# Attention with float32r score stacks in two row halves, and a normalisation moved from ScalarE to GpSimd

## The chip, the cores and the metric

The kernel runs on one core of a Trainium2 chip. The metric is the time of one execution on the device in microseconds (us), as the median of several runs. The engines are named as the profile names them: PE is TensorE (PEld its weight loads), DVE is VectorE, ACT is ScalarE, POOL is GpSimd, and SP is the engine that issues almost all DMAs of this kernel (SPq in the rows).

## The reference

Four blocks follow one another on x of shape (32, 256, 128), each as x = x + block(layernorm(x)): retention, a mixture of 16 experts with one shared, softmax attention, and a block that routes 63 tokens of each sequence through attention and an FFN. The change is in the third block and at the edge of the fourth:

```python
h = _layernorm(x, axis=-1)                 # x: 32 sequences x 256 tokens x 128
q = (h @ Wq.T + bq).reshape(b, s, 16, 8) * 8 ** -0.5
k = (h @ Wk.T + bk).reshape(b, s, 16, 8)
v = (h @ Wv.T + bv).reshape(b, s, 16, 8)
probs = softmax(einsum('bqhd,bkhd->bhqk', q, k))
x = x + einsum('bhqk,bkhd->bqhd', probs, v).reshape(b, s, 128) @ Wo.T + bo
h3 = _layernorm(x, axis=-1)                # input of the last block
```

## The kernel before, in words

`attention_phase` handles the 32 sequences in a software pipeline that is written out by hand: each engine has a list of steps with lags, and in turn `it` it runs each step of its list for sequence `it - lag`. All engines work in order, so the order of a list is the order of the work, and semaphores hold a step until its inputs are there.

A head has only 8 values, so a score matmul would use 8 of the 128 rows of the PE array. The kernel uses the rows for precision instead. `split_qk` on POOL cuts q and k into three bfloat16 parts (four dependent operations for each of q and k). `store_parts` writes the parts to DRAM and `fill(half)` reads them back into `q_stack` and `k_stack`, one row for each pair of parts and each of the 8 values: 72 rows, for 8 heads (a half) at a time. One bfloat16 matmul on 72 rows then gives the score of a head. It is computed twice. `for_maximum(j)`, called m0 to m7 below, computes four heads with queries on the partitions, and DVE reduces them to the negated maximum. `split_max` cuts the maximum into three parts, `transpose_max` turns it, `copy_maxT` takes it from PSUM, and `give_max` writes it as three more rows under `q_stack`, against rows of ones under `k_stack`. `for_exponential(j)`, e0 to e7, then gives score minus maximum with keys on the partitions, on 75 rows, and ACT takes the exponential. `values(g)`, V0 to V3, multiplies with v in four column strips of the array.

Per sequence SP issues 11 DMAs: four stores of parts, four fills, two maxima and the output. `q_stack` and `k_stack` have two buffers (p is 0 or 1), and a fill for sequence s waits until the e steps of the same half of sequence s - 2 are done, and until the parts of s are stored. PE waits for the fills at m0 (half 0) and m4 (half 1), and for the maxima at e0 and e4.

One turn of PE's list is: e6, v, m7, e7, V2, m0, oT, e0, m1, y, e1, m2, max1, V3, h, e2, m3, e3, token, V0, m4, qk, m5, e4, m6, max0, V1, e5. Here v, qk and y are projections, h, oT and token are transposes, and max0 and max1 are `transpose_max`.

SP's list of one turn:

```python
pipeline(sp, [(fill(1), 4), (fill_ones, 4), (store_parts, 3), (store_out, 9), (give_max(1), 5),
              (fill(0), 3), (give_max(0), 4), (load_later, 0)], B, B)
```

At the end of a sequence `inv_std3` on POOL computes the scale and shift of the next layernorm, `norm3` on ACT applies them (two ACTIVATEs of 128x128), and `weigh` on POOL uses the result.

Of the kernel before, what the change touches and what calls it, by code (L numbers as in the profile page):

```python
# [10 lines left out]
BF16 = mybir.dt.bfloat16  # L11
I32 = mybir.dt.int32
U32 = mybir.dt.uint32
ALU = mybir.AluOpType
# [987 lines left out]
PARTS = 3  # L1002
PAIRS = PARTS * PARTS
QK_ROWS = PAIRS * AD
EXP_ROWS = QK_ROWS + PARTS
UNIT = 4
M_UNITS = AH // UNIT * TPS
# [25 lines left out]
def attention_phase(nc, w, keep, out):  # L1033


    with Memory(nc) as m:
# [8 lines left out]
        ident_b = m.sbuf("a_ident_b", [P, P], BF16)  # L1045
# [3 lines left out]
        ones_b = m.sbuf("a_ones_b", [PARTS, S], BF16)  # L1049
# [10 lines left out]
        rest = m.sbuf("a_rest", [P, 2, S])  # L1060
        part = m.sbuf("a_part", [P, 2, 2, PARTS, S], BF16)
        SLOTS = 2 * PARTS + PARTS - 1
        part_dram = nc.dram_tensor("part_dram", (2, HALVES, SLOTS, AD, HH, S), BF16, kind="Internal").ap()
        q_stack = m.sbuf("a_q_stack", [P, 2, HALVES, HH, S], BF16)
        k_stack = m.sbuf("a_k_stack", [P, 2, HALVES, HH, S], BF16)
        v_tok = m.sbuf("a_v_tok", [P, 2, TPS, D])
        v_pad = m.sbuf("a_v_pad", [P, 2, TPS, AH, APAD])
        neg_max = m.sbuf("a_neg_max", [P, 2, HALVES, TPS, HH])
        max_rest = m.sbuf("a_max_rest", [P, TPS, HH])
        max_part = m.sbuf("a_max_part", [P, HALVES, TPS, PARTS, HH], BF16)  # L1070
        max_T = m.sbuf("a_max_T", [PARTS * HH, HALVES, S], BF16)
# [65 lines left out]
        h3_done = m.sem("e_h_done")  # L1137
        product_done = m.sem("e_product_done")
# [8 lines left out]
        FILLS = 2  # L1147
# [5 lines left out]
        def _(sp):  # L1153
# [8 lines left out]
            def fill_ones(s, p, r):  # L1162
                if s == 0:
                    sp.wait_ge(preset, 4)
                    for q in range(2):
                        for half in range(HALVES):
                            sp.dma_start(k_stack[QK_ROWS:EXP_ROWS, q, half],
                                         ones_b[:].unsqueeze(1).to_broadcast([PARTS, HH, S])).then_inc(ones_in, 16)

            def store_parts(s, p, r):  # L1170
                slots = lambda half, first, end: part_dram[p, half, first:end].rearrange("a d h s -> (d h) a s")
                rows = lambda half: part[half * HH * AD:(half + 1) * HH * AD, p].rearrange("r w a s -> r (w a) s")
                after(sp, part_step, 8 * s + 4)
# [5 lines left out]
                for half in range(HALVES):  # L1179
                    sp.dma_start(slots(half, 0, 2 * PARTS), rows(half)).then_inc(part_stored[p][half], 16)  # L1180
# [1293 lines left out]
```

## Time and profile before

| what | value |
|---|---|
| median of 3 runs | 1086.14 us (1085.76 to 1087.13) |
| the profiled execution | 1087.2 us, span of its instructions 1085.4 us |
| attention phase, first m0 to last e | 482.8 to 960 us of the span |
| busy over the whole span | PE 88%, DVE 65%, POOL 65%, ACT 59% |
| PE clock granted, mean | 0.949 of full speed |

The span is what the profile shows from the first to the last instruction. Busy shares are means over four phases with different limits. For this change only the attention phase counts, and in it the stretch in which the pipeline is full.

### The profile page before, as it was taken

To read this page: it belongs to the slowest core of one execution; us is meant where nothing else is said; L and a number is where in the kernel's file an instruction comes from. 1 tells how busy PE (TensorE), PEld (TensorE's weight loads), DVE (VectorE), ACT (ScalarE), POOL (GpSimd) and SP (SyncE) were. 2 spreads that over 40 slices of the span, in tenths; PEclk is the share of its full clock that TensorE was granted. 3 is DMA by queue.
4 is the path that set the end of the run, shared out by engine and by line. 5 is a ranking of instruction groups with operands and counts; after the bars stand their busy time and mean duration, and the time that the engine had idled before them with its cause. 6 is when DMAs were issued, how large, how long until landed. Compare 5 with 4: busy or idle time off the path is not lost. (4 is left out here: it accounts for less than half of the span.)

```text
span 1085.4 us, 29610 instructions
## 1 busy us (share of the span) xinstructions
PE 956.3 (88%) x9809; PEld 706.1 (65%) x9810; DVE 704.7 (65%) x1509; ACT 641.7 (59%) x1304; POOL 703.8 (65%) x1531
## 2 busy tenths in 40 slices
PE   6999997669899999449999999999999999954675
PEld 5888886458777666335767777777777777623554
DVE  5888887634444444237788777778878777825752
ACT  4777775311124433125788888888888888752551
POOL 4777775466625555467688888888888887544003
PEclk9999999789999999757999999999999999987999
DMA  8600000311122332134344544454454444302000
GB/s 319 252 3 3 3 3 2 121 45 42 42 70 82 82 84 65 44 109 132 116 140 138 149 127 140 125 147 137 139 141 129 125 124 128 102 16 61 7 3 20
DMA packets 88836, 100.90 MB, mean 93 GB/s; under 512 B 10654, under 2 KB 74366, under 8 KB 88318
## 3 DMA queue, kind: packets, MB, share of 16 engines
q1 hardware_dynamic: 83454, 87.98, 27.5%
q0 software_dynamic: 5248, 11.15, 3.2%
q8 instruction: 82, 1.34, 0.5%
q14 instruction: 52, 0.43, 0.1%
HBM read 61.79 MB, written 36.47 MB: 91 GB/s over the span
## 5 line engine op out<-in xcount | busy, mean ns | idle before, releaser
L1367 DVE TENSOR_REDUCE a_neg_max<-a_slot 128x4 f32<-128x1024 f32 x256 | 306.7, 1219 | 109.0 <-PE a_slot L1510 84.3
L1455 ACT ACTIVATE a_pT<-a_slot 128x1024 f32<-128x1024 f32 x256 | 255.4, 1024 | 14.0 <-PE a_slot L1526 7.1
L1510 PE MATMUL a_slot<-a_k_stack,a_q_stack 72*128 72x256 bf16 x1024 | 158.3, 279 | 7.3 <-DMA a_k_stack<-part_dram 6.5
L1526 PE MATMUL a_slot<-a_q_stack,a_k_stack 75*128 75x256 bf16 x1024 | 150.8, 275 | 2.6 <-ACT a_pT L1455 0.7
L1541 PE MATMUL a_ps_o<-a_pT,a_v_pad 128*32 128x256 f32 x2048 | 141.6, 386 | 0.0
L1510 PEld LDWEIGHTS a_slot<-a_k_stack,a_q_stack 72*128 72x128 bf16 x1024 | 95.7, 99 | 51.8 <-issue 25.5
L727 POOL DMA_INDIRECT y_rows<-m_total,m_token x80 | 76.6, 957 | 68.7 <-issue 40.4
L1526 PEld LDWEIGHTS a_slot<-a_q_stack,a_k_stack 75*128 75x128 bf16 x1024 | 92.8, 98 | 36.4 <-ACT a_pT L1455 14.3
L720 POOL DMA_INDIRECT sorted_in<-h,m_slot x64 | 62.6, 978 | 42.5 <-issue 24.0
L330 DVE TENSOR_TENSOR r_score<-ps_score,r_decay 128x512 f32<-128x512 f32 x128 | 81.5, 678 | 7.9 <-PE ps_score L489 7.8
L1541 PEld LDWEIGHTS a_ps_o<-a_pT,a_v_pad 128*32 128x32 f32 x2048 | 64.8, 109 | 27.5 <-issue 13.0
L910 PE MATMUL m_banks<-h2T,shared_up 128*128 (+1 forms) x256 | 65.3, 401 | 16.3 <-ACT m_gate L860 12.0
L829 DVE TENSOR_TENSOR m_hidden_e<-m_gate_e,m_banks 128x512 f32<-128x512 f32 x40 | 27.5, 688 | 76.2 <-issue 60.8
L959 PE MATMUL m_banks<-expert_up,m_xeT 128*128 x160 | 75.4, 593 | 0.3 <-ACT m_xeT L868 0.3
L860 ACT ACTIVATE m_gate<-m_banks 128x512 f32<-128x512 f32 x32 | 19.1, 597 | 86.8 <-PE m_banks L910 39.8
L910 PEld LDWEIGHTS m_banks<-h2T,shared_up 128*128 128x128 f32 x256 | 48.6, 199 | 25.4 <-issue 19.5
L385 ACT ACTIVATE r_h<-x,r_shift,r_rstd 128x128 f32<-128x128 f32 x128 | 56.7, 497 | 12.4 <-POOL r_shift L257 11.9
L776 DVE TENSOR_TENSOR m_hidden<-m_gate,m_banks 128x512 f32<-128x512 f32 x32 | 21.9, 685 | 53.9 <-remote 26.8
L875 ACT ACTIVATE m_gate_e<-m_banks 128x512 f32<-128x512 f32 x40 | 23.9, 598 | 48.5 <-PE m_banks L959 42.1
L255 POOL TENSOR_TENSOR r_rstd<-r_ve,r_half 128x2 f32<-128x2 f32 x64 | 45.3, 707 | 5.0
L1272 POOL TENSOR_TENSOR a_part<-a_qk,a_zeros 128x256 bf16<-128x256 f32 x64 | 39.1, 611 | 11.3 <-ACT a_qk L1441 8.8
L1272 POOL TENSOR_TENSOR a_part<-a_rest,a_part 128x256 bf16<-128x256 f32 x64 | 43.0, 672 | 5.0
(296 smaller groups left out, 2113.6 us busy)
## 6 DMA issues: line engine op xcount, KB each, us to landing
a_q_stack<-part_dram SPq DMA_DIRECT2D x64, 288.0 KB
a_k_stack<-part_dram SPq DMA_DIRECT2D x64, 288.0 KB
part_dram<-a_part SPq DMA_DIRECT2D x64, 192.0 KB, 2.7
sorted_in<-h SPq DMA_DIRECT2D x10, 528.0 KB, 13.0
m_xe<-sorted_in SPq DMA_DIRECT2D x40, 132.0 KB
expert_up<-in_eu_dram SPq DMA_DIRECT2D x1, 4096.0 KB, 24.2
part_dram<-a_part SPq DMA_DIRECT2D x64, 64.0 KB, 3.8
out_dram<-e_x_plus_h SPq DMA_DIRECT2D x32, 128.0 KB, 2.5
```

Of the source, the lines that this page charges most:

```text
L330: nc.vector.tensor_tensor(score[:, p, tile], ps_score[tile][:], own, ALU.mult).then_inc(score_done, 1)
L385: ins = nc.scalar.activation(h[:, p, t], x_sb[:, s * TPS + t, :], ACT.Identity, bias=shift[:, p, t:t + 1], scale=rstd[:, p, t:t + 1])
L720: nc.gpsimd.indirect_dma_start(sorted_in, bass.IndirectOffsetOnAxis(ap=slot[:, t:t + 1], axis=0), h2_all[:, t, :], None).then_inc(scattere ...
L727: nc.gpsimd.indirect_dma_start(y_rows, bass.IndirectOffsetOnAxis(ap=token[:, at:at + 1], axis=0), ye[:, t % RING, j], None).then_inc(store ...
L910: ins = nc.tensor.matmul(bank[2 * which + p][:, f * S:(f + 1) * S], shared_up[:, which, f], h2T_all[:, bass.ds(s * S, S)], start=True, sto ...
L959: ins = nc.tensor.matmul(bank[PAIR * (p % 2) + j], xeT[:, p % 2, j], w_up[:, expert[j]], start=True, stop=True)
L1272: nc.gpsimd.tensor_tensor(to, a, b, op).then_inc(steps, 1)
L1367: nc.vector.tensor_reduce(neg_max[:, p, half, t, g * UNIT:(g + 1) * UNIT], slots[SLOT_OF["m", j]][:], AX.X, ALU.max, negate=True).then_inc ...
L1455: nc.scalar.activation(pT[:, j % PT_RING], slots[SLOT_OF["e", j]][:], ACT.Exp).then_inc(e_read, 1)
L1510: ins = nc.tensor.matmul(slots[SLOT_OF["m", j]][:, q], q_stack[0:QK_ROWS, p, half, head, t * P:(t + 1) * P], k_stack[0:QK_ROWS, p, half, h ...
L1526: ins = nc.tensor.matmul(slots[SLOT_OF["e", j]][:, q], k_stack[0:EXP_ROWS, p, half, head, t * P:(t + 1) * P], q_stack[0:EXP_ROWS, p, half, ...
L1541: ins = nc.tensor.matmul(ps_o[q * APAD:(q + 1) * APAD, g // 2], v_pad[:, p, t, g * UNIT + q], pT[:, (2 * g + t) % PT_RING, q], start=g % 2 ...
```

## The change

- The scores use float32r operands. q and k are cut into two parts instead of three (two POOL operations each instead of four), so that the pairs of parts take 4 x 8 = 32 rows.
- The stacks are float32 and hold two halves of rows. Rows 0 to 63 serve one half of the heads of a group and rows 64 to 127 the other. In each half rows 32 to 61 are filled with zeros on both sides, and rows 62 and 63 hold the two parts of the maximum on the q side and ones on the k side. The m matmuls use 62 rows of a half and the e matmuls 64. The matmuls of a group of four heads alternate between the two row halves, and write two PSUM banks.
- The DRAM scratch is split into `q_dram` and `k_dram`. Per sequence there are six stores of parts, eight fills of 32 rows, four maxima of 2 rows, and the output: 19 DMAs instead of 11.
- The k fill reads its 16 rows twice by an outermost dimension of 2 with step 0. The q fill repeats in an inner dimension, as before.
- `norm3` runs on POOL as two whole-tile operations with broadcast scale and shift.
- The one-off fill of zeros and ones is larger and stands first in SP's list.

```diff
-PARTS = 3
+PARTS = 2
-EXP_ROWS = QK_ROWS + PARTS
+TILES = 2
+TILE_ROWS = P // TILES
+MAX_ROWS = TILE_ROWS - PARTS
+HT = HH // TILES
...
             def fill(half):
                 def step(s, p, r):
                     after(sp, e_filled, ((s - 2) * 4 + 2 * half + 2) * (M_UNITS // 8) * 2)
-                    after(sp, part_stored[p][half], twice(16, r + 1))
-                    sp.dma_start(q_stack[0:QK_ROWS, p, half],
-                                 part_dram[p, half, 0:PARTS].rearrange("a d h s -> (a d) (h s)").unsqueeze(1)
-                                 .to_broadcast([PARTS * AD, PARTS, HH * S])).then_inc(filled[p][half], 16)
-                    sp.dma_start(k_stack[0:QK_ROWS, p, half],
-                                 bass.AP(part_dram.tensor, part_dram[p, half, PARTS].offset,
-                                         [[HH * S, PARTS * AD], [AD * HH * S, PARTS], [1, HH * S]])
-                                 ).then_inc(filled[p][half], 16)
+                    after(sp, part_stored[p][half], 16 * STORES * (r + 1))
+                    for tile in range(TILES):
+                        rows, heads = slice(tile * TILE_ROWS, tile * TILE_ROWS + QK_ROWS), slice(tile * HT, (tile + 1) * HT)
+                        sp.dma_start(q_stack[rows, p, half],
+                                     q_dram[p, half, :, :, heads].rearrange("a d h s -> (a d) (h s)").unsqueeze(1)
+                                     .to_broadcast([PARTS * AD, PARTS, HT * S])).then_inc(filled[p][half], 16)
+                        sp.dma_start(k_stack[rows, p, half],
+                                     k_dram[p, half, :, :, heads].rearrange("d a h s -> (d a) (h s)").unsqueeze(0)
+                                     .to_broadcast([PARTS, PARTS * AD, HT * S])).then_inc(filled[p][half], 16)
...
+            def scores(slot, rows, weights, moving, of_weights, p, half, g):
+                for r in range(UT):
+                    for tile in range(TILES):
+                        at = slice(tile * TILE_ROWS, tile * TILE_ROWS + rows)
+                        ins = nc.tensor.matmul(slot[:, tile * UT + r], weights[at, p, half, g * UT + r, of_weights].bitcast(F32R),
+                                               moving[at, p, half, g * UT + r].bitcast(F32R), start=True, stop=True)
...
+            def norm3(s, p, r):
+                after(pool, shift3_done, s + 1)
+                h3 = given[:, bass.ds(s * TPS, TPS), 0:D]
+                over_d = lambda a: a[:, p].unsqueeze(2).to_broadcast([P, TPS, D])
+                nc.gpsimd.tensor_tensor(h3, x_sb[:, bass.ds(s * TPS, TPS), :], over_d(rstd3), ALU.mult).then_inc(scaled3, 1)
+                after(pool, scaled3, s + 1)
+                nc.gpsimd.tensor_tensor(h3, h3, over_d(shift3), ALU.add).then_inc(h3_done, 1)
```

SP's instructions for one turn in the full pipeline, from `fill(1)` to `give_max(0)`; first before (sizes are partitions x repeats x elements):

```order
L1187 DMA a_q_stack<-part_dram 72x1x2048
L1190 DMA a_k_stack<-part_dram 72x1x2048
L1176 DMA part_dram<-a_part 64x2x256 x2
L1180 DMA part_dram<-a_part 64x6x256 x2
L1206 DMA out_dram<-e_x_plus_h 128x2x128
L1199 DMA a_q_stack<-a_max_T 3x8x256
```

The turn goes on with the same fills for half 0 and one more maximum. And after the change, the whole turn:

```order
L1198 DMA a_q_stack<-q_dram 32x1x1024
L1201 DMA a_k_stack<-k_dram 32x1x1024
L1198 DMA a_q_stack<-q_dram 32x1x1024
L1201 DMA a_k_stack<-k_dram 32x1x1024
L1184 DMA k_dram<-a_part 8x8x256 x4
L1188 DMA q_dram<-a_part 64x2x256 x2
L1219 DMA out_dram<-e_x_plus_h 128x2x128
L1211 DMA a_q_stack<-a_max_T 2x4x256 x2
L1198 DMA a_q_stack<-q_dram 32x1x1024
L1201 DMA a_k_stack<-k_dram 32x1x1024
L1198 DMA a_q_stack<-q_dram 32x1x1024
L1201 DMA a_k_stack<-k_dram 32x1x1024
```

Each fill of a half has become four issues, the stores six, and each maximum two, all in the same place of the turn; a pair of maxima follows as before.

POOL's instructions for one turn, from the bias to the output, before:

```order
L1237 TENSOR_TENSOR x<-x,a_bo 128x256
L1300 TENSOR_TENSOR a_v_pad<-a_v_tok,a_zeros 128x4x4x8 x2
L1252 TENSOR_TENSOR e_shift<-e_minus_mean,e_rstd 128x2
L1272 TENSOR_TENSOR a_max_part<-a_neg_max,a_zeros 128x2x8
L1272 TENSOR_TENSOR a_max_rest<-a_neg_max,a_max_part 128x16
L1272 TENSOR_TENSOR a_max_part<-a_max_rest,a_zeros 128x2x8
L1272 TENSOR_TENSOR a_max_part<-a_max_rest,a_max_part 128x2x8
L1311 TENSOR_TENSOR e_product<-h,d_rw 128x256
```

And after:

```order
L1251 TENSOR_TENSOR x<-x,a_bo 128x256
L1313 TENSOR_TENSOR a_v_pad<-a_v_tok,a_zeros 128x4x4x8 x2
L1266 TENSOR_TENSOR e_shift<-e_minus_mean,e_rstd 128x2
L1324 TENSOR_TENSOR h<-x,e_rstd 128x2x128
L1326 TENSOR_TENSOR h<-h,e_shift 128x2x128
L1284 TENSOR_TENSOR a_max_part<-a_neg_max,a_zeros 128x4x4
L1286 TENSOR_TENSOR a_max_part<-a_neg_max,a_max_part 128x4x4
L1332 TENSOR_TENSOR e_product<-h,d_rw 128x256
```

The two operations of `norm3` (on `h`) have come in right behind the shift, and the split of a maximum has two operations instead of four. The order of the matmul groups on PE is the same in both kernels.

## Rows read from the trace of the kernel before

**Rows 1.** The page, part 1: busy time of each engine.

```profile
PE 956.3 (88%) x9809; PEld 706.1 (65%) x9810; DVE 704.7 (65%) x1509; ACT 641.7 (59%) x1304; POOL 703.8 (65%) x1531
```

**Rows 2.** Windows, full pipeline: stretch, length, engines' busy us, PE clock, DMA share, GB/s.

```profile
641.20:935.60 294.40, 293.63 (x3054) 207.85 (x3057) 236.27 (x391) 243.76 (x418) 250.09 (x590) 1.00 0.48 134
```

**Rows 3.** Groups of DVE and POOL instructions in 641.2 to 935.6 us.

```profile
L1367 DVE TENSOR_REDUCE a_neg_max<-a_slot 128x4 f32<-128x1024 f32 x161 | 192.9, 1219 | 57.7 <-PE a_slot L1510 41.4 <-POOL a_max_part L1272 15.0
L1377 DVE TENSOR_TENSOR a_o_tok<-a_ps_misc,a_inv_sum 128x256 f32<-128x256 f32 x20 | 8.5, 424 | 0.7
...
L1311 POOL TENSOR_TENSOR e_product<-h,d_rw 128x256 f32<-128x256 f32 x20 | 14.5, 726 | 1.6
```

**Rows 4.** Timeline of PE inside one turn: start us, length us, engine, line.

```profile
707.07 0.60 PE L1510 MATMUL a_slot<-a_k_stack,a_q_stack 72*128 72x256 bf16 x4
707.50 0.60 PE L1526 MATMUL a_slot<-a_q_stack,a_k_stack 75*128 75x256 bf16 x4
...
710.59 0.59 PE L1596 MATMUL a_ps_misc<-a_hT,a_wk 128*128 128x256 f32 x2
711.02 0.60 PE L1510 MATMUL a_slot<-a_k_stack,a_q_stack 72*128 72x256 bf16 x4
```

**Rows 5.** Timeline of PE in the retention phase, with a matmul group in row strips.

```profile
101.86 0.38 PE L527 MATMUL ps_tail<-ident,r_h 128*128 128x128 f32 x2
102.17 1.15 PE L489 MATMUL ps_score<-r_qT,r_kT 32*128 32x256 f32 x16
103.24 1.08 PE L504 MATMUL ps_turns<-r_score,r_v_pad 128*32 128x128 f32 x32
```

**Rows 6.** Timeline of POOL: a split of q, of which two steps stand here.

```profile
703.30 0.61 POOL L1272 TENSOR_TENSOR a_part<-a_qk,a_zeros 128x256 bf16<-128x256 f32 x1
704.00 0.67 POOL L1272 TENSOR_TENSOR a_rest<-a_qk,a_part 128x256 f32<-128x256 f32 x1
...
706.19 0.73 POOL L1237 TENSOR_TENSOR x<-x,a_bo 128x256 f32<-128x256 f32 x1
```

**Rows 7.** Timeline of SP's DMA issues in one turn.

```profile
701.19 0.79 SPq L1187 DMA_DIRECT2D a_q_stack<-part_dram  x1
...
703.51 1.31 SPq L1176 DMA_DIRECT2D part_dram<-a_part  x2
706.14 1.24 SPq L1180 DMA_DIRECT2D part_dram<-a_part  x2
707.42 0.65 SPq L1206 DMA_DIRECT2D out_dram<-e_x_plus_h  x1
708.13 0.79 SPq L1199 DMA_DIRECT2D a_q_stack<-a_max_T  x1
709.03 0.84 SPq L1187 DMA_DIRECT2D a_q_stack<-part_dram  x1
709.92 0.77 SPq L1190 DMA_DIRECT2D a_k_stack<-part_dram  x1
```

**Rows 8.** Waits of SP in 641.2 to 935.6: us in total, times, longest.

```profile
SPq L1199 <- ACT a_max_T L1447: 45.1, 20, 2.7
SPq L1180 <- POOL a_part L1272: 36.2, 20, 1.9
SPq L1187 <- PE a_slot L1526: 32.9, 21, 1.9
```

**Rows 9.** Issues of 128-partition loads at the program's start: min/median/max ns.

```profile
L221 SPq DMA_DIRECT2D x<-in_x_dram x4: 398/432/432, 0.8 to 7.8; - x4
```

**Rows 10.** Windows with full DMA queues: a 128-partition load, then fills alone.

```profile
20.00:25.00 5.00, 5.00 (x80) 4.15 (x69) 4.60 (x16) 2.90 (x8) 1.92 (x7) 1.00 1.04 418
479.20:479.40 0.20, 0.00 (x0) 0.00 (x0) 0.00 (x0) 0.06 (x1) 0.20 (x2) 0.50 0.80 328
```

**Rows 11.** The page, part 3: SP's queue over the span.

```profile
q1 hardware_dynamic: 83454, 87.98, 27.5%
```

**Rows 12.** Line 1176, the smaller store of parts.

```profile
DMA to landing us min/median/max: 2.2/3.8/5.0
```

More of the change, by code:

```diff
@@ L1170, in store_parts @@
             def store_parts(s, p, r):
-                slots = lambda half, first, end: part_dram[p, half, first:end].rearrange("a d h s -> (d h) a s")
-                rows = lambda half: part[half * HH * AD:(half + 1) * HH * AD, p].rearrange("r w a s -> r (w a) s")
-                after(sp, part_step, 8 * s + 4)
+                rows = lambda half, which: part[half * HH * AD:(half + 1) * HH * AD, p, which]
+                after(sp, part_step, 2 * PARTS * s + PARTS)
                 for half in range(HALVES):
@@ L1175, in store_parts @@
                     after(sp, filled[p][half], twice(8 * FILLS, r))
-                    sp.dma_start(slots(half, 2 * PARTS, SLOTS), rows(half)[:, PARTS:2 * PARTS - 1]
+                    for a in range(PARTS):
+                        sp.dma_start(k_dram[p, half, :, a], rows(half, 1)[:, a]
+                                     ).then_inc(part_stored[p][half], 16)
+                after(sp, part_step, 2 * PARTS * (s + 1))
+                for half in range(HALVES):
+                    sp.dma_start(q_dram[p, half].rearrange("a d h s -> (d h) a s"), rows(half, 0)
@@ L1177, in store_parts @@
                                  ).then_inc(part_stored[p][half], 16)
-                after(sp, part_step, 8 * (s + 1))
-                for half in range(HALVES):
-                    sp.dma_start(slots(half, 0, 2 * PARTS), rows(half)).then_inc(part_stored[p][half], 16)
             def fill(half):
@@ L1280, in step @@
                         for half in range(HALVES):
-                            after(pool, part_stored[p][half], twice(16, r))
-                    split(part_step, 8 * s + 4 * n, qk[:, p, which], rest[:, which], part[:, p, which, 0],
-                          part[:, p, which, 1], part[:, p, which, 2], [P, S])
+                            after(pool, part_stored[p][half], 16 * STORES * r)
+                    split(part_step, 2 * PARTS * s + PARTS * n, qk[:, p, which], part[:, p, which, 0], part[:, p, which, 1], [P, S])
                 return step
@@ L1632, in by_half @@
 def by_half(weight):
-    return np.ascontiguousarray(weight.reshape(-1, HALVES, HH, AD).transpose(0, 1, 3, 2).reshape(-1, D))
+    heads = weight.reshape(-1, HALVES, HH // UNIT, TILES, UT, AD)
+    return np.ascontiguousarray(heads.transpose(0, 1, 5, 3, 2, 4).reshape(-1, D))
 def by_pair(rows):
```

120 lines of the change are left out of this document (57 added, 63 removed).

## The prediction

> **What bounds the kernel now.** I read the page's busy times first: PE leads with 88% [rows 1]. That is a mean over four phases, so the next view is the windows of the stretch in which the attention pipeline is full. In 294.4 us PE is busy 293.6 us at full clock, POOL 250.1, ACT 243.8, DVE 236.3, and the DMA engines 48% [rows 2]. The groups of the same stretch contain exactly 20 multiplications of `a_o_tok`, one per sequence [rows 3], so one turn takes 294.4 / 20 = 14.72 us. Per turn PE is busy 14.68 us, POOL 12.5, ACT 12.2, DVE 11.8. DVE's reduction of the maxima waited 41.4 us for PE [rows 3]: PE ends last, and the others follow. SP is not in those columns. Its own waits add up to 45.1 + 36.2 + 32.9 = 114.2 us over the 20 turns, 5.7 us each [rows 8], so its 11 issues take the other 9.0 us. SP is an in-order engine with 5.7 us to spare, and the change gives it 19 issues.
>
> **The change part by part.**
>
> *PE, less work in the scores.* A bfloat16 group of four heads takes 0.44 us from its start to the next group's [rows 4], and a turn has 16 of them. No float32r matmul is in the trace. Its lower bound is the bfloat16 price, its upper bound that of float32: there a matmul of 256 columns, in two records, takes 0.43 us [rows 4] where bfloat16 takes 0.11. That row strips run beside each other is shown by the retention scores: 16 float32 records in four strips take 1.07 us until the next group starts [rows 5], where 16 records in sequence at 0.43 / 2 would take 3.4. Two strips thus halve a group: 0.22 us at the bfloat16 rate, 0.86 at the float32 rate. I take the bfloat16 rate, because the kernel cuts the values into parts ahead, as it does for bfloat16 and for no float32 matmul; the saving is 16 x 0.22 = 3.5 us a turn.
>
> The Trainium skill (FP8 and Floating Point Precision, TensorE Precision Notes) says that true float32 takes four passes and that there is a reduced form which reads 4-byte values and truncates them. By it the lower end would hold; no row of this trace shows it.
>
> *PE, more changes of the array's division.* In rows 5 the two transposes (0.22 us, as a record of 128 columns takes 0.43 / 4) last 0.31 us until the strips start: 0.09 us for the change. The strip group takes 1.07 us where four rounds of 0.215 are 0.86, of which 0.09 is the next change and about 0.11 the first weight load, which is hidden nowhere. So a change into 128-column work costs 0.2 us. In PE's list the division changes 8 times a turn before (around the `values` groups, with max0 and max1 in the same strips as V3 and V1), and 18 times after, because each projection or transpose now stands between strip groups. That is 10 x 0.2 = 2.0 us more, and 4 x 0.1 for the float32r load that is now unhidden at the four old changes from `values` back to scores or transposes. PE: 14.7 - 3.5 + 2.0 + 0.4 = 13.6 us.
>
> *POOL.* A split of q lasts from 703.30 to 706.19, 2.9 us, of which the first two operations take 0.70 and about 0.65 [rows 6]. Each of the two splits saves 1.5 us, each split of a maximum about 0.6. `norm3` adds two operations of 0.73 [rows 3] and a wait of 0.08. Net 12.5 - 3.0 - 1.2 + 1.5 = 9.8 us. ACT loses two ACTIVATEs. Both stay under 13.6 us, so these parts move nothing by themselves; the cover is PE's (or SP's) turn, and without it the moved normalisation would cost its 1.5 us.
>
> *SP.* From issue to issue a store takes 0.66 us (1.31 for two), the output 0.71, a maximum 0.90, a fill 0.89 [rows 7]. After: 6 x 0.66 + 0.71 + 4 x 0.90 + 8 x 0.89 = 15.4 us a turn. The lower bound takes the q fills at the price of plain loads, 0.43 us [rows 9], plus a gap of 0.05: 4 x 0.41 less, 13.8 us. SP no longer has its 5.7 us, and behind each issue stand all later fills and maxima, for which PE waits at m0, m4, e0 and e4.
>
> *The fills' spread.* This term decides. When only fills are queued, the DMA engines are 80% busy and move 328 GB/s, where a load of 128 partitions fills them (1.04) and moves 418 [rows 10]. The fills' 72 rows begin with a dimension of 24, and 0.8 of 16 engines is about 12, half of 24. So a fill is not spread over all engines, and what it is spread over follows its dimensions, not its bytes. The new k fill's source begins with a dimension of 2 (the repeat with step 0). If the outermost dimension limits the spread, two engines carry the 32 rows of 4 KB, the same two for each k fill. The bounds are 16 engines and 2. I take 2, as the dimension is nearest to that.
>
> The Trainium skill (DMA: Bandwidth & Descriptors, "Why a DMA increments its semaphore by 16 and not by 1") states this as a rule: the number of engines is the largest up to 16 that divides the slowest dimension of both access patterns. By it the fills of before have 12 engines, with which the trace's 0.80 agrees, and the new k fills 2, the lowest-numbered. That speaks against this change.
>
> *Price with two engines.* 328 GB/s over 12 engines are 27.3 bytes per ns, so a 4 KB row takes 0.15 us and a k fill 16 x 0.15 = 2.4 us. The page gives the slow bound: 87.98 MB in 27.5% of 16 engines' 1085.4 us are 18.4 bytes per ns [rows 11], 3.6 us a k fill. The pair's ring is in order, so the loop of one turn is: both k fills of half 1 with the q rows between, 5.1 us; the stores issued behind them, about 1.2; their completion, 0.8; SP sees `part_stored` and issues a q and a k fill of half 0, 1.8; start-up, 0.8; the k fills of half 0, 5.1; q rows and the maxima behind them, 0.6; semaphores and gaps, 0.5. Start-up plus completion is 1.6 because a small store lands 2.2 us after an issue of 0.63 at best [rows 7, 12]. Sum 15.9 us. At the slow price each of four k fills costs 1.2 more: 20.6 us.
>
> **Sum.** The loop (15.9) is longer than SP's issues (13.8 to 15.4) and PE's work (13.6). A turn grows by 1.2 us, 32 turns by 39 us. Ahead of the first m0 the fills are 3 us slower and two splits 3 us faster: nothing. The profiled execution took 1087.2 us, of which 1085.4 is span; 1087.2 + 39 = 1126, and the median of the runs lies 1.1 us lower: 1125. I round up to 1127, as every in-order wait of SP adds to the loop.
>
> **The rivals.**
> - *Wide spread, cheap issues: faster.* If a k fill runs on four or more engines, it takes at most 1.2 us and the loop falls below SP's time. With q fills issued at 0.43 us the turn is SP's 13.8 with a little waiting, 13.9: 32 x 0.8 = 26 us less, about 1060; with still cheaper issues PE's 13.6, 1050. For it: nothing in the trace shows a repeat dimension in front. Against: the 0.80 share, and SP's sum. It decides at an SP turn of 14.7 us. Chance 0.17; a tie within 0.2% (2 us, what a measurement of this kernel can tell from no change), a turn of 14.66 to 14.78, has 0.04.
> - *Wide spread, SP's issues at full price.* The turn is 15.4 us: 32 x 0.7 = 22, 1108. Chance 0.10.
> - *float32r is not at the bfloat16 rate.* At half of it PE's turn is 13.6 + 3.5 = 17.1, 1163; at the float32 rate 13.6 + 16 x 0.64 = 23.8, 1377. Chances 0.08 and 0.05.
> - *PE's clock falls in the new waits.* While PE stood idle before m0 the granted clock was 0.50 [rows 10], and 1.00 in the full pipeline [rows 2]. With a turn of 15.9 PE waits 2.3 us, in pieces at m0, e0 and e4. If half of each turn ran at half clock, 13.6 would become 20.4: 1270. Short waits speak against. Chance 0.04.
>
> **The numbers.** The narrow loop has 0.52, with its own range from 1108 (SP's full price) to 1175 (part of the rows at the slow price). Predicted 1127 us. The range goes from 1065 to 1190: it leaves out the lower half of the fast rival and, above, the float32 rate, the clock and the slow end of the loop, 0.2 together. Faster 0.17, same 0.04, slower 0.79.
>
> **What would show it.** SP's waits nearly gone but for `part_stored` and the e steps; a DMA share that falls though the bytes stay; PE idle before m0 and e0 with the k fill or the maximum as releaser; groups of four heads 0.22 us apart; DVE and ACT less busy per turn. I am wrong if a full-pipeline turn is under 14.7 us, if PE waits for nothing and still takes longer, or if the score groups take 0.4 us or more.

## The result and the profile after

The changed kernel takes 1207.46 us (median of 4 runs, 1200.32 to 1220.06), the kernel before 1086.64 on the same chip. The ratio is 1.108, with a 95% interval of 1.102 to 1.114: slower by 121 us where 41 were predicted, and above the range (1190). The ratio leaves out the slowest of the four, 1220.06 us, which is the profiled one; its mean granted clock, 0.899, is that of the other three (0.896 to 0.902), so its rows are used for where the time goes and the ratios for how much.

The page, part 1 and the largest idle times of part 5 (columns after the bar: busy us and mean ns, idle us ahead of the group and its releaser):

```profile
PE 982.5 (81%) x9810; PEld 686.2 (56%) x9810; DVE 708.4 (58%) x1508; ACT 619.8 (51%) x1240; POOL 633.0 (52%) x1340
...
L1387 DVE TENSOR_REDUCE a_neg_max<-a_slot 128x4 f32<-128x1024 f32 x256 | 308.1, 1221 | 211.3 <-PE a_slot L1518 204.4
...
L1518 PE MATMUL a_slot<-a_k_stack,a_q_stack 62*128 62x256 f32 x1024 | 129.7, 338 | 93.0 <-DMA a_k_stack<-k_dram 91.2
```

PE is busy for longer than before [rows 1] although its matmuls were to become shorter, and it waits 93 us ahead of the m groups, nearly all of it for the k fill. DVE, whose work is the same [rows 3], now waits 204 us for PE.

The window of the full pipeline, which is [rows 2] for the kernel before, and the multiplication of `a_o_tok` in it, one per sequence (number, durations in ns, first and last start):

```profile
535.50:1071.00 535.50, 446.03 (x4408) 277.29 (x4400) 344.15 (x563) 330.93 (x542) 292.50 (x668) 0.91 0.33 99
```

```profile
L1397 DVE TENSOR_TENSOR a_o_tok<-a_ps_misc,a_inv_sum x30: 424/424/426, 535.5 to 1071.0; 128x256 f32<-128x256 f32 x30
```

A turn takes 535.5 / 29 = 18.47 us on average, in place of 14.7. (The median execution is 12.6 us shorter than the profiled one; if the difference lies in the 32 turns, its turn is 0.4 us less, by estimate 18.1.) PE is busy 15.38 us of it and idle 3.09, and its clock, 1.00 before, is 0.91. The average hides a pattern. The starts of that multiplication in a row, from DVE's timeline:

```profile
759.36 0.42 DVE L1397 TENSOR_TENSOR a_o_tok<-a_ps_misc,a_inv_sum 128x256 f32<-128x256 f32 x1
773.83 0.42 DVE L1397 TENSOR_TENSOR a_o_tok<-a_ps_misc,a_inv_sum 128x256 f32<-128x256 f32 x1
796.60 0.42 DVE L1397 TENSOR_TENSOR a_o_tok<-a_ps_misc,a_inv_sum 128x256 f32<-128x256 f32 x1
811.09 0.42 DVE L1397 TENSOR_TENSOR a_o_tok<-a_ps_misc,a_inv_sum 128x256 f32<-128x256 f32 x1
834.23 0.42 DVE L1397 TENSOR_TENSOR a_o_tok<-a_ps_misc,a_inv_sum 128x256 f32<-128x256 f32 x1
```

14.5, 22.8, 14.5, 23.1 us: every second turn is as fast as before the change, and the other loses 8. What the slow one is made of stands in windows of PE (length, busy us, granted clock, DMA share, GB/s) and in two rows of its timeline:

```profile
780.00:782.50 2.50, 2.50 (x32) 1.00 0.22 57
782.50:785.00 2.50, 0.71 (x16) 1.00 0.35 107
785.00:787.50 2.50, 0.67 (x5) 0.94 0.39 120
787.50:790.00 2.50, 2.50 (x14) 0.50 0.64 180
790.00:792.50 2.50, 2.50 (x20) 0.50 0.30 98
792.50:795.00 2.50, 2.50 (x29) 0.70 0.16 53
```

```profile
786.83 0.50 PE L1518 MATMUL a_slot<-a_k_stack,a_q_stack 62*128 62x256 f32 x4 [3.62 <-DMA a_k_stack<-k_dram]
...
791.86 1.93 PE L1553 MATMUL a_ps_o<-a_pT,a_v_pad 128*32 128x256 f32 x16
```

PE works without a pause until 783, stands still for 3.62 us ahead of m0 until the k fill has landed, and goes on. Only then does the clock fall, from 1.00 to 0.50 (from 2.4 to 1.2 GHz). The windows' clocks put it at 0.50 for 0.3 + 5.0 + 1.5 = 6.8 us. A group of values that takes 1.07 us elsewhere takes 1.93 there. So the slow turn pays twice, once for the wait and once for what the wait does to the clock. A wait of 1.38 us for the other half's k fill, ahead of the m4 at 812.71, leaves the clock at 1.00. Why slow and fast turns alternate is not shown. The half speed may give the transfers time to catch up, but it is not needed for it: in `warm6` below, turns of 16.0 and 19.0 us alternate in places where the clock did not fall.

### The profile page after: what moved, and what is told of

Its sections match the earlier page's. It is cut to its first block and busy times, and to the rows that moved or that the text cites. A ratio compares the mean times of both kernels' runs of the same rounds, so it can differ in the third digit from the quotient of the medians.

```text
span 1218.2 us, 29542 instructions
## 1 busy us (share of the span) xinstructions
PE 982.5 (81%) x9810; PEld 686.2 (56%) x9810; DVE 708.4 (58%) x1508; ACT 619.8 (51%) x1240; POOL 633.0 (52%) x1340
## 3 DMA queue, kind: packets, MB, share of 16 engines
q8 instruction: 82, 1.34, 0.5%
## 5 line engine op out<-in xcount | busy, mean ns | idle before, releaser
L1518 PE MATMUL a_slot<-a_k_stack,a_q_stack 62*128 62x256 f32 x1024 | 129.7, 338 | 93.0 <-DMA a_k_stack<-k_dram 91.2
L1518 PEld LDWEIGHTS a_slot<-a_k_stack,a_q_stack 62*128 62x128 f32 x1024 | 89.3, 214 | 136.9 <-DMA a_k_stack<-k_dram 103.0
L1553 PE MATMUL a_ps_o<-a_pT,a_v_pad 128*32 128x256 f32 x2048 | 146.2, 406 | 0.0
L1518 PE MATMUL a_slot<-a_q_stack,a_k_stack 64*128 64x256 f32 x1024 | 124.6, 335 | 14.0 <-DMA a_q_stack<-a_max_T 11.1
L1518 PEld LDWEIGHTS a_slot<-a_q_stack,a_k_stack 64*128 64x128 f32 x1024 | 82.2, 202 | 51.4 <-issue 23.3
L1313 POOL TENSOR_TENSOR a_v_pad<-a_v_tok,a_zeros 128x128 f32<-128x128 f32 x64 | 24.2, 398 | 155.6 <-PE a_ps_o L1553 155.6
L1553 PEld LDWEIGHTS a_ps_o<-a_pT,a_v_pad 128*32 128x32 f32 x2048 | 55.7, 114 | 52.9 <-issue 28.6
L386 ACT ACTIVATE r_h<-x,r_shift,r_rstd 128x128 f32<-128x128 f32 x128 | 56.7, 497 | 12.4 <-POOL r_shift L258 11.9
L1284 POOL TENSOR_TENSOR a_max_part<-a_neg_max,a_zeros 128x16 fp32r<-128x16 f32 x64 | 13.7, 213 | 91.8 <-DVE a_neg_max L1387 91.8
L1460 ACT ACTIVATE a_qk<-a_ps_misc,a_bq_scaled 128x256 f32<-128x256 f32 x32 | 15.2, 474 | 76.9 <-PE a_ps_misc L1608 76.9
L1488 ACT COPY a_oT<-a_ps_misc 128x256 f32<-128x256 f32 x32 | 11.9, 372 | 74.9 <-PE a_ps_misc L1622 74.6
```

What stands on the lines that cost most here:

```text
L386: ins = nc.scalar.activation(h[:, p, t], x_sb[:, s * TPS + t, :], ACT.Identity, bias=shift[:, p, t:t + 1], scale=rstd[:, p, t:t + 1])
L1313: ins = nc.gpsimd.tensor_tensor(own_columns(v_pad[:, p].rearrange("p t h e -> p (t h) e"), g), v_tok[:, p].rearrange("p t (a g q e) -> p ( ...
L1518: ins = nc.tensor.matmul(slot[:, tile * UT + r], weights[at, p, half, g * UT + r, of_weights].bitcast(F32R), moving[at, p, half, g * UT + ...
L1553: ins = nc.tensor.matmul(ps_o[q * APAD:(q + 1) * APAD, g // 2], v_pad[:, p, t, g * UNIT + q], pT[:, (2 * g + t) % PT_RING, q], start=g % 2 ...
```

## The experiments

Theory A, formed on these rows: each k fill is carried by two of the 16 DMA engines, their ring makes the fills late, and the clock comes on top. Theory B: SP's 19 issues in order are the bound. Theory C: the float32r groups in row strips make the clock fall by themselves. All ratios are to the kernel before on the same chip. Times in us that an expectation names are on the scale of the first chip (1086.64 us for before), so a ratio is what they are held against. The kernels ran on more than one chip: before takes 1065 to 1066 us on three of them and 1089 on the fourth (that of the second set), hence the ratios. Its turn is the same [rows 2] (14.68 in `before_here`). Kernels of the same turn end their first turn at 497 us on the one and at 515 on the other, so the difference lies ahead of the attention. In the kernel before and its regrouped control, whose code is the same up to there, it lies in one place: the 64 transfers to `sorted_in` in the mixture of experts start at 207.5 and 208.0 us, and the last starts at 307.4 in `before_here`, on the slower chip, and at 290.4 in `before_regroup`. Why is open.

**wide.** Part k0 is stored twice in DRAM, so that the k fill needs no repeat.

```diff
-k_dram = nc.dram_tensor("k_dram", (2, HALVES, AD, PARTS, HH, S), F32, kind="Internal").ap()
+k_dram = nc.dram_tensor("k_dram", (2, HALVES, PARTS + 1, AD, HH, S), F32, kind="Internal").ap()
...   # the two k stores of a half now write slots 0 and 1 in one transfer, and slot 2 (k0) in the other
-    k_dram[p, half, :, :, heads].rearrange("d a h s -> (d a) (h s)").unsqueeze(0)
-    .to_broadcast([PARTS, PARTS * AD, HT * S])).then_inc(filled[p][half], 16)
+    bass.AP(k_dram.tensor, k_dram[p, half, 0, 0, tile * HT].offset,
+            [[HH * S, PARTS * AD], [AD * HH * S, PARTS], [1, HT * S]])).then_inc(filled[p][half], 16)
```

> The changed kernel with the same number of issues, bytes and semaphores, but the part k0 is stored twice in DRAM (slots k0, k1, k0), so that the source of each k fill begins with a dimension of 16 instead of 2 and has no repeat. Theory A (narrow ring: two DMA engines carry each k fill, PE waits for it in every second turn and then runs at half clock): both the waits and the half clock go; a turn falls from 18.6 to between 13.6 and 14.7 us, 1050 to 1087 us in all. Theory B (SP's 19 issues in order are the bound, the spread is harmless): nothing changes, 1200 to 1215. Theory C (the score groups in row strips by themselves make the clock fall, whoever waits): the k fill waits go but the clock stays near 0.9, 1150 to 1190.

Measured: 1063.18 us, ratio 0.999 (0.9975 to 1.0007). The window of its full pipeline:

```profile
497.35:903.60 406.25, 391.91 (x4210) 246.36 (x4204) 327.91 (x541) 316.51 (x525) 284.57 (x646) 1.00 0.48 134
```

A turn is 14.65 us and the clock 1.00. SP has the same 19 issues, and the groups are the same: A holds, B and C fall. The edit also touches the k stores: their targets begin with a dimension of 64 in place of 8, and two of the four carry twice the bytes. That the k fill's source counts, and not the stores, is shown by the next two kernels: `both_narrow` keeps the new stores and has the loss, and `split` keeps the old ones, and PE waits for the k fill only 3.3 us in 430 in its weight loads, where it was 89.1 in 535.5.

**both_narrow.** From `wide`, the first two source dimensions of both fills exchanged:

```diff
-    [[HH * S, PARTS * AD], [AD * HH * S, PARTS], [1, HT * S]]
+    [[AD * HH * S, PARTS], [HH * S, PARTS * AD], [1, HT * S]]
```

> As the first kernel of this set, but with the two source dimensions exchanged in both fills, so that the q fill too begins with a dimension of 2: same bytes, same issues, eight fills a turn on two engines instead of four. Theory A: the pair carries 8 x 2.4 = 19.2 us of rows a turn, with the stores and latencies 22 to 25 us, and PE's half clock on top: 1400 to 1560 us. Theories B and C: no change from the changed kernel, 1200 to 1215.

Measured: 1394.41 us, ratio 1.308 (1.305 to 1.312), which is 1422 us on the expectation's scale, and a turn of 24.9 us, as A said. PE's windows show the ring naked:

```profile
804.00:805.00 1.00, 1.00 (x19) 1.00 0.13 53
805.00:806.00 1.00, 0.26 (x8) 1.00 0.13 53
806.00:807.00 1.00, 0.00 (x0) 1.00 0.13 53
```

The next to last column is the share of 16 engines: 0.13 is two of them, fully busy for microseconds while PE stands still. They move 53 GB/s, 26.5 bytes per ns each, so a row of 4096 bytes takes 0.155 us. The Trainium skill (DMA: Bandwidth & Descriptors, "Why a DMA increments its semaphore by 16 and not by 1") counts the engines by the slowest dimension of both patterns, here 2; the trace agrees.

**split.** The other way to a wide source: a k fill as two transfers of 16 rows.

```diff
-sp.dma_start(k_stack[rows, p, half], ... .unsqueeze(0).to_broadcast([PARTS, PARTS * AD, HT * S]))
+for n in range(PARTS):
+    sp.dma_start(k_stack[rows.start + n * PARTS * AD:rows.start + (n + 1) * PARTS * AD, p, half], ...)
```

> The changed kernel with each k fill cut into two transfers of 16 rows, one for each repeat, so that the source begins with a dimension of 16; four issues a turn more (23 in place of 19). Theory A: SP issues 12.2 + 4 x 0.6 = 14.6 us a turn, which is now the longest: 1075 to 1110 us. Theory B: four more issues make it worse, 1207 + 32 x 2.4, about 1280. Theory C: 1150 to 1200.

Measured: 1103.27 us, ratio 1.039 (1.032 to 1.047), 1129 us on the expectation's scale: far from B's 1280, but above A's range. The turn is 15.85 us, since SP with 23 issues is now the bound. These are all its waits over 27 turns:

```profile
SPq L1198 <- PE a_slot L1519: 15.4, 18, 3.4
SPq L47 <- DMA q_dram<-a_part: 0.5, 1, 0.5
```

SP works 15.3 us a turn, not 14.6. The cost of its issues is a rival to be taken seriously, but it decides at 23 of them, not at 19.

**norm_alone.** The kernel before with only `norm3` on GpSimd:

```diff
-for t in range(TPS):
-    ins = nc.scalar.activation(given[:, s * TPS + t, 0:D], x_sb[:, s * TPS + t, :], ACT.Identity, ...)
+nc.gpsimd.tensor_tensor(h3, x_sb[:, bass.ds(s * TPS, TPS), :], over_d(rstd3), ALU.mult).then_inc(scaled3, 1)
+after(pool, scaled3, s + 1)
+nc.gpsimd.tensor_tensor(h3, h3, over_d(shift3), ALU.add).then_inc(h3_done, 1)
```

> The kernel before with only the second part of the change: the normalisation ahead of the experts on GpSimd. All theories: POOL's 12.5 us a turn becomes 14.0, still under PE's 14.7, and nothing moves: 1084 to 1090 us. Rival: POOL at 14.0 hands its splits on late and PE waits for them: the 1.5 us show in every turn, up to 1135.

Measured: 1089.94 us, ratio 1.024 (1.022 to 1.027). The expectation fell and its rival held: a turn takes 15.6 us, 0.9 of the 1.5 us more, for instance 15.66 from 704.09 to 719.77 in POOL's timeline, and POOL never waits in it:

```profile
704.09 0.61 POOL L1312 TENSOR_TENSOR h<-x,e_rstd 128x256 f32<-128x256 f32 x1
704.78 0.61 POOL L1314 TENSOR_TENSOR h<-h,e_shift 128x256 f32<-128x256 f32 x1
...
719.77 0.61 POOL L1312 TENSOR_TENSOR h<-x,e_rstd 128x256 f32<-128x256 f32 x1
```

```profile
561.50:925.00 363.50, 346.43 (x3541) 240.69 (x3537) 276.93 (x464) 264.80 (x442) 323.17 (x746) 1.00 0.44 128
```

The window gives POOL 323.17 us busy in 363.50, or 13.9 a turn, and yet it is full. The missing 1.7 us are gaps of about 0.08 us between operations that wait for one another, as 704.70 to 704.78 here, which no wait is put down to. In the kernel before, POOL's 12.5 us [rows 2] plus such gaps are by this estimate 14.2 of 14.7: the cover was half a microsecond, not two.

**before_here, wide_act, four_stores_act, four_stores_pool.** The first is the kernel before, for a trace on the second chip. The second is `wide` with `norm3` back on ScalarE, as before the change. The third and fourth also store the parts of a half with two transfers instead of three, as before the change; they differ in the place of `norm3`.

```diff
-for a in range(PARTS): sp.dma_start(k_dram[...], ...)   # and q_dram, three stores for each half
+sp.dma_start(slots(half, 2 * PARTS, 2 * PARTS + 1), rows(half)[:, PARTS:PARTS + 1])   # k0 again
+sp.dma_start(slots(half, 0, 2 * PARTS), rows(half))                                   # q0 q1 k0 k1
```

> The kernel before, unchanged, for a trace of it from the chip of these runs: the ratio is 1.00 by any theory. The last set measured 1065 us for it, the runs shown at first 1086. If the difference lies in the phases ahead of the attention, its turn is 14.6 to 14.7 us here too, and the first turn ends near 497 us in place of 518.

> The changed kernel with the wide k fills (k0 stored twice) and the normalisation ahead of the experts back on ScalarE: the stacks' half of the change alone, mended. Theory A (POOL's own chain has room again once the splits are short): the normalisation's place does not matter here, a turn of 14.5 us as with the wide fills, ratio 0.996 to 1.001. Rival (POOL's two extra operations still delay the splits): a turn of 14.2 us, ratio 0.985 to 0.992.

> As the kernel with wide fills and the normalisation on ScalarE, with q and k parts stored by one transfer for each half as before (4 store issues a turn, not 6; 17 issues in all). With wide fills SP's 12.2 us of issues and its waits chain into the maxima that PE waits for (e0, 0.4 us in most turns). If SP's in-order list is what keeps the turn at 14.5 where PE needs 14.0: a turn of 14.1 to 14.3, ratio 0.985 to 0.993. If PE's work in row strips is the bound: no change against wide_act.

> The whole change, mended: wide k fills, four stores, the normalisation on GpSimd as in the change. In the kernel before that move by itself cost 2.4%, since POOL's list, 12.5 us busy and some 1.7 us of gaps, had under 0.5 us to spare. Here the splits are 4.2 us shorter. If that is the whole reason: as four_stores_act, 0.990 to 0.997. If the move also costs through the order of POOL's list: 1.000 to 1.010.

Measured: `before_here` 1085.8 us. `wide_act` 0.9995 (0.997 to 1.002). `four_stores_act` 0.994 (0.991 to 0.996), `four_stores_pool` 0.993 (0.991 to 0.996). `wide_act` and `wide` do not differ, nor do the last two: the place of `norm3` does not matter once the splits are short. With 17 issues the mended change is faster than the kernel before by 0.6 to 0.7%, which is small, but the intervals leave out 1. The windows of `four_stores_act`:

```profile
517.36:895.00 377.64, 366.12 (x3965) 231.16 (x3958) 308.82 (x514) 315.38 (x545) 241.32 (x565) 1.00 0.49 137
```

The turn is 14.48 us, with PE busy 14.04 and POOL 9.3. In `wide_act` it is 14.70. So SP's list took 0.2 us a turn, but the turn of 14.1 to 14.3 that was expected if it were the whole distance to PE's work did not come.

**warm and warm6.** The changed kernel, narrow fills and all, with useless work where PE would stand idle: 12 or 6 float32 multiplications into the free bank of m0, ahead of the wait.

```diff
+free_slot("m", j, s)
+if j == 0:
+    for n in range(12):   # 6 in warm6
+        nc.tensor.matmul(slots[SLOT_OF["m", j]][:, n % UNIT, 0:P], wq[:], wk[:], start=True, stop=True)
 if j % 4 == 0:
     after(pe, filled[p][half], 16 * FILLS * (r + 1))
-free_slot("m", j, s)
```

> The changed kernel with its narrow k fills, and 12 useless float32 multiplications of 128 columns (2.6 us of PE) written to the free bank of m0 ahead of the wait for the fill, so that PE does not stand idle there. If the half clock after the wait of 3.7 us is a real part of the loss: the clock stays at 1.00, the turns no longer alternate between 14.5 and 22.7, each takes 16.5 to 18 us, 1165 to 1190 us at this chip's before of 1086 (ratio 1.06 to 1.10). If the clock is only a by-product and the ring is all: the added work costs its 2.6 us where PE did not wait, ratio 1.13 to 1.16.

> As warm (narrow fills, useless multiplications ahead of m0's wait), with 6 in place of 12, 1.3 us. PE's work is then 14.5 + 1.3 = 15.8 us a turn. If the ring of the narrow fills by itself needs about 15.9 us, as the prediction said, and the clock stays up: turns of 16.0 to 16.6, ratio 1.045 to 1.065. If the ring itself needs more (17 and above): ratio 1.08 to 1.10, with PE waiting for the k fill in each turn. If 1.3 us are too little to keep the clock: alternating turns, 1.09 to 1.12.

Measured: `warm` 1186.47 us, ratio 1.091 (1.089 to 1.094), `warm6` 1.094 (1.088 to 1.099), both with less time than the changed kernel's 1.108 although PE has 2.9 or 1.4 us more to do in each turn. The window and the work itself in `warm`:

```profile
528.50:1014.00 485.50, 468.15 (x4863) 321.34 (x4855) 325.58 (x537) 313.44 (x523) 284.01 (x646) 1.00 0.35 105
```

```profile
711.81 2.94 PE L1530 MATMUL a_slot<-a_wk,a_wq 128*128 128x128 f32 x24
714.68 0.50 PE L1518 MATMUL a_slot<-a_k_stack,a_q_stack 62*128 62x256 f32 x4
```

The clock stays at 1.00, the turns no longer alternate (17.59 us on average), and m0 follows the useless work directly, with the k fill already there, as the expectation's first case said. So the half clock was a real part of the loss, and the narrow fills alone can be served in 17.6 us. In `warm6` the turn averages 17.96 us, and two of its turns, as windows, tell wait and clock apart:

```profile
564.00:583.00 19.00, 15.85 (x172) 10.36 (x164) 11.96 (x20) 11.47 (x20) 10.53 (x25) 1.00 0.32 98
...
635.20:656.60 21.40, 18.62 (x172) 11.76 (x164) 11.96 (x21) 11.70 (x20) 10.87 (x25) 0.84 0.31 90
```

Both have 172 records of PE and about 3 us of idle time. At clock 1.00 they take 15.85 us of PE, at a mean of 0.84 18.62: 2.8 us of clock in one turn. Not every idle stretch costs clock, and its length alone does not decide. These are the waits of two m0:

```profile
628.18 0.50 PE L1518 MATMUL a_slot<-a_k_stack,a_q_stack 62*128 62x256 f32 x4 [2.25 <-DMA a_k_stack<-k_dram]
...
792.89 0.50 PE L1518 MATMUL a_slot<-a_k_stack,a_q_stack 62*128 62x256 f32 x4 [1.69 <-DMA a_k_stack<-k_dram]
```

After the longer one the clock is 1.00 up to 640 us. After the shorter one it is 0.76 on average from 792.9 to 800.0, with half clock from 794.3 on. The changed kernel has one such case too: a wait of 1.65 us ahead of the m0 at 878.18, and a clock of 0.57 from 879 to 883. What else decides was not measured. The expectation for 6 multiplications (16.0 to 16.6 us a turn if the ring needs 15.9) fell. The time lies in both of its other cases, a ring of 17 us and more with a wait for the k fill in nearly every turn, and a clock that falls in some of them.

**serial_strips, one_strip, full_rows.** The last question is PE's own work. All three start from `four_stores_act`.

```diff
-for r in range(UT):            # serial_strips: these two loops exchanged
-    for tile in range(TILES):
-        at = slice(tile * TILE_ROWS, tile * TILE_ROWS + rows)
+        at = slice(0, rows)    # one_strip
+        at = slice(0, P)       # full_rows
```

> four_stores_act with the two loops of a score group exchanged: two matmuls of the first row half, then two of the second, where they alternate else. Same work, same data, same bank writes. If alternating halves run side by side and two of the same half do not, a group inside a run takes 0.35 to 0.44 us in place of 0.24, a turn grows by 16 x 0.1 to 0.2: ratio 1.08 to 1.20. If the saving of a group came from the float32r form and not from the strips: no change from four_stores_act, 0.992 to 0.996.

> four_stores_act with all four matmuls of a score group on the first row half (rows 0 to 61 or 63), so that no two of them can lie side by side; the scores of the other half's heads are left out (the first half's stand in their place). Same count, columns and form. If the saving of a group comes from the two halves side by side: a group inside a run takes 0.44 us in place of 0.24, a turn 14.5 + 16 x 0.2 = 17.7 us, ratio 1.08 to 1.09. If it comes from the float32r form or the smaller number of rows: no change, 0.991 to 0.996.

> four_stores_act with all four matmuls of a score group over all 128 rows, so that the array's division changes only around the values groups, as before; each score is then the sum of two heads', and the maxima are multiplied by 0 (these parts of the computation are left out). A group should take 4 x 0.11 = 0.44 us as in bfloat16 before. If each change of division costs about 0.2 us (2.0 us a turn for ten): one_strip's turn less 2 us, 14.7 to 15.7 us, ratio 1.00 to 1.03. If the changes are nearly free and the strips gain little by themselves: as one_strip, 1.07 or more.

Measured: `serial_strips` 0.991 (0.988 to 0.994), `one_strip` 1.088 (1.085 to 1.091), `full_rows` 1.025 (1.022 to 1.029). The first came out close to what its expectation gave for a saving from the float32r form (0.992 to 0.996). But it does not separate the two, since in it a matmul of the first half can still lie beside the next one of the second. The other two do: `one_strip` has the form and loses the saving. Windows of `one_strip` and of `full_rows` (turns of 17.47 and 15.64 us):

```profile
508.20:962.50 454.30, 454.30 (x3964) 324.88 (x3956) 310.37 (x514) 321.16 (x544) 242.09 (x565) 1.00 0.41 114
```

```profile
496.80:903.00 406.20, 406.20 (x3952) 321.01 (x3948) 306.21 (x511) 318.11 (x542) 240.97 (x562) 1.00 0.46 127
```

PE is never idle in either, so a turn is PE's work. One after the other: from before to `full_rows` (float32r form, float32 transposes of the maxima, no strips) 14.68 to 15.64, +0.96 us; to `one_strip` (the division changes) 17.47, +1.83; to `four_stores_act` (the halves side by side) 14.04 of PE's work, -3.43. Of the first, 16 x 0.04 = 0.64 us lie in the groups, which start 0.48 us apart in `full_rows` (at 682.24, 682.72 and 683.20) where it was 0.44 [rows 4]. With it goes a change in the weight loads, here of `full_rows`:

```profile
L1515 PEld LDWEIGHTS a_slot<-a_q_stack,a_k_stack 128*128 128x128 f32 x1024 | 136.6, 190 | 21.4 <-issue 14.6
```

190 ns for 128 columns. The bfloat16 loads of the unchanged scores take about half of that, here in the page of `norm_alone`:

```profile
L1511 PEld LDWEIGHTS a_slot<-a_k_stack,a_q_stack 72*128 72x128 bf16 x1024 | 96.4, 100 | 51.4 <-issue 25.5
```

The Trainium skill (TensorE: Matmul & The Clock Gate, Weight-path perf modes) names no gain from the fast weight load for fp32; the pair of numbers fits, if float32r counts as such. That the loads are what makes a group 0.04 us longer is argued, not shown: no run changes them alone. The Trainium skill also says (TensorEngine Tiling (Array Packing), Key Properties) that changing the mode drains the engine: 1.83 us for ten changes, 0.18 each, agree with that.

**regroup and before_regroup.** If a change of division costs 0.18 us, fewer visits should pay.

```diff
-(for_exponential(6), 5), (project_v, 2), (for_maximum(7), 4), (for_exponential(7), 5),
-(values(2), 5), (for_maximum(0), 3), (transpose_o, 6), (for_exponential(0), 4),
+(for_exponential(6), 5), (for_maximum(7), 4), (for_exponential(7), 5), (project_v, 2),
+(values(2), 5), (transpose_o, 6), (for_maximum(0), 3), (for_exponential(0), 4),
```

> four_stores_act with two steps of PE moved so that fewer changes of the array's division are left: the projection of v from between e6 and m7 to directly before the values group V2, and the transposes of o from between m0 and e0 to directly behind V2. If the changes between row strips and full work are what ate the strips' saving (a group alone takes 0.34 us plus some 0.4 in leaving, against 0.24 inside a run), two visits fewer save 2 x 0.3 us a turn: 13.9 us in place of 14.5, ratio 0.973 to 0.982. If the turn is bound elsewhere (the misc bank's chain of copies, ACT, DVE): no change, 0.990 to 0.996; if the steps' waits now stand in PE's way: slower than that.

> A control for the regrouping: the same two moves in the kernel before, where the scores are not in strips, so that no change of division goes away: 0.998 to 1.002. If the moves help there as much as in the other kernel, their gain there has nothing to do with the division.

Measured: 1.018 (1.015 to 1.020), and 1.019 (1.016 to 1.022) for the control. Both turns are 15.4 us. The window of `regroup`:

```profile
498.20:898.90 400.70, 359.20 (x3952) 225.54 (x3948) 305.83 (x511) 316.58 (x543) 240.85 (x562) 1.00 0.46 129
```

The moves take away two changes of division in a turn, 0.37 us at 0.18 each. PE is busy 13.8 us a turn, 0.2 less than 14.04, so there is a little to gain. But PE now waits for the banks of the score slots:

```profile
689.04 0.50 PE L1515 MATMUL a_slot<-a_q_stack,a_k_stack 64*128 64x256 f32 x4 [0.65 <-ACT a_pT L1464]
```

The order that was there spaces the score groups as ACT and DVE free their slots; packed together, they wait. Against `four_stores_act` the moves cost 2.4% (1.018 against 0.994), and in the control 1.9%, so most of the loss has nothing to do with the strips.

## Why the prediction was right and wrong

**Direction and cause: right.** The fills' spread was called the term that decides, two engines were chosen from bounds of 2 and 16, and `wide`, `both_narrow` and `split` show that it is two and that without it the loss of 10.8% is gone. The price of a row (0.15 us taken, 0.155 measured) was right as well.

**The step that failed is the sum of the loop.** It put a turn at 15.9 us; 18.47 were measured. There are two parts:

- *The loop without the clock.* In the changed kernel PE is busy 15.38 us a turn, 1.34 more than the 14.04 of the same work in `four_stores_act`. Less that, 18.47 gives 17.1 us, an estimate, since a PE that is faster may also wait longer; `warm`, where the clock stays, bounds it at 17.6. The prediction's terms are 1.2 to 1.7 us short. The row price explains 0.3 (64 rows by 0.005). A further part is the stores behind the k fills, for which 1.2 us were taken. SP had issued the k fills of half 1 by 805.60 and the stores behind them by 809.54. This is a window of PE while SP waits for those stores, and the packets in nearly the same stretch:

```profile
812.20:814.20 2.00, 1.49 (x8) 1.00 0.15 50
...
DMA packets 88, 0.08 MB, mean 47 GB/s; under 512 B 10, under 2 KB 88, under 8 KB 88
```

  A k fill's rows are packets of 4 KB. These 78 between 512 B and 2 KB in 1.7 us are the stores' rows of 1 KB, and again only about two engines are busy (0.15), for some 2.0 us, with 14 idle: the stores' share on the pair that carries the k fills comes last. That is 0.8 more than the term. SP waits for it, 36.9 us in 25 turns, and sends the fills of half 0 only then:

```profile
SPq L1211 <- ACT a_max_T L1467: 90.7, 42, 4.1
SPq L1198 <- PE a_slot L1518: 37.5, 41, 1.3
SPq L47 <- DMA q_dram<-a_part: 36.9, 25, 3.4
```

- *The clock.* The prediction had it as a rival of chance 0.04, with "Short waits speak against." It summed the wait of 2.3 us a turn in pieces. In fact most of it comes in one piece, in every second turn, of 3.6 us in the rows above and of 3.2 to 4.5 in all but one, and then the clock does fall. It adds 1.34 us a turn to PE's work, not the 6.8 of that rival, and to the turn, against `warm`, which does more work, at least 0.6 by the ratios (0.017 of 1087 us over 32 turns) and 0.9 by the profiles (18.47 less 17.59). The rival and the main case were both true at once, which a list of exclusive cases has no place for.

**The start: wrong.** "Nothing" was taken. The first turn ends at 535.5 us, at 518.2 before and at 514.7 in `wide_act` on a chip of the same speed. The larger one-off fill is not the reason, since `wide_act` has it too. The first k fills are narrow, and up to 535 us PE waits four times for one, 21.6 us in all. Before, PE is at half clock there too, but leaves it sooner. The same ten microseconds, before and after:

```profile
500.00:510.00 10.00, 10.00 (x83) 6.49 (x81) 4.99 (x7) 6.02 (x9) 5.38 (x14) 0.78 0.38 102
...
500.00:510.00 10.00, 4.27 (x28) 3.00 (x27) 3.71 (x5) 2.16 (x4) 3.68 (x9) 0.50 0.62 151
```

Together: in the profiled execution the 31 intervals between the 32 turns took 558 us in place of 448 (+110), the start +17, the end +5.

**PE: 13.6 us predicted, 14.04 of work and 14.48 with its waits.** The strips' saving was right (3.5 taken, 3.43 measured) and so were the division changes (2.0, 1.83). Float32r was mis-sized: +0.4 taken, +0.96 measured. Its rate was taken from bfloat16, while a group without strips takes 0.04 us more and each of its weight loads nearly twice as long. That also made the fast rival too good: it gave 1060 us, 0.976, for a wide spread, where `wide` measured 0.999 and the version with fewer stores 0.993.

**SP: right that it does not bound, for the wrong reason.** Its issues were put at 13.8 to 15.4 us a turn; in one turn after they are:

```profile
803.73 0.62 SPq L1201 DMA_DIRECT2D a_k_stack<-k_dram  x1
804.39 0.57 SPq L1198 DMA_DIRECT2D a_q_stack<-q_dram  x1
805.00 0.60 SPq L1201 DMA_DIRECT2D a_k_stack<-k_dram  x1
805.70 2.54 SPq L1184 DMA_DIRECT2D k_dram<-a_part  x4
808.27 1.27 SPq L1188 DMA_DIRECT2D q_dram<-a_part  x2
809.59 0.59 SPq L1219 DMA_DIRECT2D out_dram<-e_x_plus_h  x1
810.23 1.41 SPq L1211 DMA_DIRECT2D a_q_stack<-a_max_T  x2
```

8 fills of 0.60, stores of 2.54 and 1.27, the output, and four maxima in 2.7 to 2.8: about 12.2 with the gaps. A fill of 32 rows is cheaper than one of 72 (0.77 to 0.84, [rows 7]), and a maximum of 2 rows takes 0.7 where one of 3 rows and twice the heads took 0.79. "SP's waits nearly gone" was therefore wrong too: 175 us are left over 29 turns, 6.0 a turn, where it was 5.7 [rows 8].

**The normalisation: right for the changed kernel, wrong as argued.** "The cover is PE's turn" holds with `four_stores_pool` and `four_stores_act` (0.993 and 0.994), but only because the splits shrank in the same change. Against the kernel before it costs 2.4%. POOL's own sum was near: 9.8 us a turn taken, 10.1 measured (292.50 / 29).

**The signs named** held for PE idle before m0 with the k fill as releaser, for a DMA share of 0.33 in place of 0.48, and for DVE and ACT as shares of the turn: they are busy 11.9 and 11.4 us of 18.47 where it was 11.8 and 12.2 of 14.7. Groups 0.22 apart: 0.24 inside a run, as the four rows' starts show, from `four_stores_act`.

```profile
703.25 0.50 PE L1515 MATMUL a_slot<-a_q_stack,a_k_stack 64*128 64x256 f32 x4
703.59 0.40 PE L1515 MATMUL a_slot<-a_k_stack,a_q_stack 62*128 62x256 f32 x4
703.83 0.40 PE L1515 MATMUL a_slot<-a_q_stack,a_k_stack 64*128 64x256 f32 x4
704.24 0.63 PE L1598 MATMUL a_ps_misc<-ident,a_oT_pad 128*128 128x128 f32 x4
```

The first of a run takes 0.34 and the last 0.41 until the next step: the average over a turn is well above 0.24.

**What stays open:** what of an idle stretch makes the clock fall (waits of 1.65 to 2.65 us are of both kinds); why slow and fast turns alternate; how the 17.1 us of the ring divide beyond the terms above; and why the transfers to `sorted_in` take some 17 us longer on some chips.

## What to carry to other kernels

A repeat of rows in a DMA's source belongs in an inner dimension, or the repeated part is stored twice: here an outermost dimension of 2 left 14 of 16 DMA engines idle (a share of 0.13), and a profile shows it as a DMA share near 2/16 while an engine waits. When a new wait is priced, ask whether it comes in one piece and what PE's clock does behind it, since the two add up. And an engine's slack is its turn less busy time and less the gaps between its dependent operations, which on POOL, with some 32 operations a turn in `norm_alone`, came to 1.7 us that no column shows.

## What was not expected of the hardware

- A wait of 3.62 us on a PE that had been busy throughout was followed by 6.8 us at half clock, while waits of 1.4 us were not, and ones of 1.65 to 2.65 us were in part. Useless matmuls in the wait made the kernel faster, from 1.108 to 1.091.
- The same loop of transfers gave turns of 14.5 and 22.8 us by turns: a mean over turns describes neither.
- Float32r weight loads take 190 ns for 128 columns, bfloat16 ones 100; a group of four matmuls without strips takes 0.48 us in place of 0.44.
- An issue of SP takes 0.6 us for a fill of 32 rows and about 0.8 for one of 72.
